# A graph layer in fp32: every gather of node rows is given a bound on its indices

## What is computed

```python
ea  = edge_attr @ w_e + b_e                        # (E, 64) @ (64, 256)
msg = relu(x[src] + ea)                            # one row of x per edge
agg = segment_sum(msg, dst, num_segments=N)        # sum of a node's edges
t = x + agg
h_local = bn(relu(t @ w1 + b1) @ w2 + b2 + x)
# attention inside groups of 32 nodes, 4 heads of 64 channels
q, k, v = split(x.reshape(256, 32, 256) @ in_w.T + in_b)
h_attn = bn(softmax(q k^T / 8) v @ out_w.T + out_b + x)
out = h_local + h_attn
out = bn(out + relu(out @ m_w1 + m_b1) @ m_w2 + m_b2)
return layernorm(x + out)
```

## Time and profile before

| what | value |
|---|---|
| median of 3 runs | 1321.83 us (1321.43 to 1322.18) |
| profiled execution, first to last instruction | 1321.8 us |
| PE busy with matmuls | 1242.6 us, 94% |
| POOL busy | 970.7 us, 73% |
| DVE busy | 819.9 us, 62% |
| ACT busy | 552.5 us, 42% |
| mean granted clock of TensorE | 0.977 of full speed |

### The profile page before, as it was taken

One profiled execution on the slowest core, in us unless ns is written; L12 is line 12 of the kernel. 1 busy time (PEld: TensorE's weight loads), 2 busy tenths in 40 slices (PEclk: granted clock), 3 DMA queues, 4 the chain that ended last, 5 costly groups with the idle time before them and its releaser, 6 DMA issues.

```text
span 1321.8 us, 21000 instructions
## 1 busy us (share of the span) xinstructions
PE 1242.6 (94%) x7307; PEld 729.6 (55%) x7307; DVE 819.9 (62%) x1831; ACT 552.5 (42%) x1077; POOL 970.7 (73%) x1032
## 2 busy tenths in 40 slices
PE   5797999999999999999999999999999999999997
PEld 3454555555555555555555545555455556767676
DVE  4757456657475575746667475575746657548554
ACT  1343434444344434444443444443444434444443
POOL 7777777777777777777777777777777777777760
PEclk7897999999999999999999999999999999999999
DMA  9454645555555555555555555555555555545540
GB/s 325 137 177 144 180 136 160 170 173 177 158 155 168 170 169 162 177 160 162 170 162 177 152 156 167 170 170 155 162 176 164 168 158 155 184 146 151 178 140 18
DMA packets 113259, 216.02 MB, mean 163 GB/s; under 512 B 21505, under 2 KB 62721, under 8 KB 113153
## 3 DMA queue, kind: packets, MB, share of 16 engines
q0 software_dynamic: 49152, 134.28, 35.1%
q1 hardware_dynamic: 62560, 77.09, 18.1%
q10 hardware_dynamic: 1440, 3.29, 0.7%
HBM read 197.80 MB, written 16.78 MB: 162 GB/s over the span
## 4 chain that ended last, share of the span: by engine, by line
PE 55%; POOL 19%; DVE 11%; issue 9%; DMA 4%; DVEq 1%; ACT 1%
PE bank L746 28%; POOL xg L368 19%; PE bank L774 12%; PE bank L789 11%; DMA xg<-in_x_dram,srcs 4%; DVE bank L592 3%; PE bank L798 2%; DVE mx L635 2%; DVE dif L640 1%; PE bank L871 1%; PE bank L845 1%; DVEq L608 1%; DVE o L667 1%; DVE aggT L624 1%; DVE probT L656 1%
## 5 line engine op out<-in xcount | busy, mean ns | idle before, releaser
L368 POOL DMA_INDIRECT xg<-in_x_dram,srcs x1024 | 969.8, 947 | 313.5 <-issue 297.0
L393 ACT ACTIVATE msg<-bank 128x512 f32<-128x512 f32 x512 | 277.7, 594 | 392.7 <-PE bank L774 392.2
L592 DVE TENSOR_TENSOR bank<-xg,bank 128x512 f32<-128x512 f32 x512 | 337.3, 690 | 157.8 <-DMA xg<-in_x_dram,srcs 132.4
L774 PE MATMUL bank<-we,ea 64*128 64x256 f32 x2048 | 297.8, 410 | 55.5 <-DVE bank L592 55.5
L774 PEld LDWEIGHTS bank<-we,ea 64*128 64x128 f32 x2048 | 182.0, 190 | 205.4 <-issue 146.8
L789 PE MATMUL bank<-msg,onehot 128*64 128x256 f32 x2048 | 254.7, 392 | 4.0 <-DVE aggT L624 4.0
L789 PEld LDWEIGHTS bank<-msg,onehot 128*64 128x64 f32 x2048 | 139.8, 139 | 103.7 <-issue 47.8
L624 DVE TENSOR_TENSOR aggT<-bank,aggT 128x128 f32 x256 | 74.7, 292 | 187.4 <-PE bank L798 142.7
L746 PE MATMUL bank<-xT,iwT 128*128 128x512 f32 x256 | 125.8, 614 | 6.6 <-DMA xT<-in_xT_dram 6.6
L746 PE MATMUL bank<-o,m 128*128 128x512 f32 (+2 forms) x352 | 122.8, 483 | 0.0
L746 PE MATMUL bank<-h,m 128*128 128x512 f32 (+2 forms) x352 | 116.8, 479 | 1.0 <-ACT h L453 1.0
(11 more groups left out here) (88 smaller groups left out, 927.0 us busy)
## 6 DMA issues: line engine op xcount, KB each, us to landing
ea<-in_ea_dram SPq DMA_DIRECT2D x128, 256.0 KB
xg<-in_x_dram,srcs POOLq DMA_INDIRECT x1024
xT<-in_xT_dram SPq DMA_DIRECT2D x32, 256.0 KB, 3.9
aggT<-in_xT_dram SPq DMA_DIRECT2D x32, 256.0 KB, 5.0
oT_dram<-oT SPq DMA_DIRECT2D x32, 256.0 KB
xn<-in_x_dram SPq DMA_DIRECT2D x32, 256.0 KB, 5.1
out_dram<-xn SPq DMA_DIRECT2D x30, 256.0 KB, 2.8
m<-in_m_dram ACTq DMA_DIRECT2D x2, 512.0 KB, 17.9
```

Of the source, the lines that this page charges most:

```text
L368: pool.indirect_dma_start(xg[:, q % NX, n * C:(n + 1) * C], None, t["x"], bass.IndirectOffsetOnAxis(k.srcs[:, at:at + 1], 0)).then_inc(s_x ...
L393: nc.scalar.activation(msg[:, q % NM, :], EA[q % 4][:, :], ACT.Relu).then_inc(s_msg, 1)
L592: nc.vector.tensor_tensor(EA[q % 4][:, :].rearrange("p (a c) -> p a c", a=2), xg[:, q % NX, :].rearrange("p (a c) -> p a c", a=2), KB[:, 0 ...
L774: ins = nc.tensor.matmul(EA[(2 * d + pair) % 4][:, two * C:(two + 1) * C], ea[rows, n % NEA, at:at + P], k.we[rows, :], start=False, stop= ...
```

## The change

Each gather in the loop of POOL is given `bounds_check=N - 1`, that is 8191, and `oob_is_err=False`: an index above 8191 is left out of the transfer, with no error raised. Before, no bound was given, and `oob_is_err` had its default, true. No index is above 8191, so nothing is left out. Buffers, order, waits and all other engines stay.

```diff
                     pool.indirect_dma_start(
                         xg[:, q % NX, n * C:(n + 1) * C], None,
                         t["x"],
-                        bass.IndirectOffsetOnAxis(k.srcs[:, at:at + 1], 0)
+                        bass.IndirectOffsetOnAxis(k.srcs[:, at:at + 1], 0),
+                        bounds_check=N - 1, oob_is_err=False
                     ).then_inc(s_xg[q % NX], 16)
```

## The result

The changed kernel takes 1373.84 us (median of 4 runs, 1372.88 to 1374.57) against 1322.01 us (1321.43 to 1322.33): a ratio of 1.0392, 95% interval 1.0379 to 1.0405. It is 51.8 us slower. The forecast was 1348.0 us, with a range from 1308 to 1447 us; the profiled span grew from 1321.8 to 1372.8 us, by 51.0 us.

What follows compares the result with a forecast made beforehand. POOL's gathers, a full conveyor at 1.252 us each, were taken as the bound where DVE waits for them. 872 x 0.03 = 26.2 us on 1321.8 us gave 1348.0 us, range 1308 to 1447 us.

Steps and rivals of the forecast that it cites:

- The bound of the kernel: Gathers on POOL: a full conveyor, 1024 x 1.252 = 1282 us of 1321.8 us, despite its 73% busy share.
- d: What one gather on POOL becomes longer, from its start to the next one's start; taken as 0.03 us.
- the slack: At the end, the last seed's lag behind its gather beyond a waiting seed's: 6.4 - 1.9 = 4.5 us.
- What d does to the end: End moves by the larger of 872 x d and 1024 x d - 4.5 us; both 26.2 us.
- the first rule: Gathers before the last DVE seed that waits, near 1097.84 us: end moves by at least 872 x d.
- The price of d: Per gather, 0.03 us: one instruction through POOL's sequencer, and a quarter of a 0.127 us whole pass over the indices.
- The wait that moves: Ahead of each gather, the free-buffer wait moves to the register move in front; costed at nothing.
- Hidden: Rival: move read under the running gather, comparison made anyway; d below 3 ns, time 1321.8 us; chance 0.27.
- A pass of its own: Rival: inside each gather, POOL goes over the 128 indices again, up to 0.127 us; up to 1447.3 us; chance 0.16.
- The error path goes away: Rival: gathers lose 0.03 us of error bookkeeping; gain 13.7 us over 455 gathers, to 1308.1 us; chance of faster 0.14.
- Cut-up transfers: Rival: gathers' queue goes from 48 to 144 packets per gather; beyond 1600 us; 0.07 together with a much slower gather.
- The signs to look for: Line of gathers: gap above 0.30 us means the move or its wait; median above 946 ns means the check.

## Why the prediction was right, and where it was off

**The bound of the kernel.** Right. POOL at 73% busy was a full conveyor, and d x 1024 less a part of the slack came out at the end.

**What d does to the end.** Right. With the measured d of 0.053 us, 1024 x 0.053 - 4.5 = 49.8 us; the span grew by 51.0 us. The slack gave back 3.5 us, not 4.5, since the last seed stayed 2.9 us behind its gather and not 1.9. The run with the bound on the early gathers bears out the first rule, 46 us expected and 45 measured. The late ones show that the slack swallows a part, 3.5 us expected and 4.9 measured in the repeat; as in the changed kernel, it seems to give back less than 4.5 us.

**The price of d.** This term was mis-sized: 0.03 us taken, 0.053 us measured, 26 us forecast and 51 us found. The reason that carried it was mostly wrong in kind. It was the price of one more instruction through the sequencer. The moves do cost 29 ns each, close to the spacing of the memsets, but they lie under the gathers; with one move in place of 1024 the time is the same. The price is inside the gather and nearly fixed. The second reason, a fraction of the 0.127 us that stood for a pass, pointed at the right place, but the fraction of a quarter was picked and not read from a row; it came out as 0.4. (The 0.127 us were not the smallest instruction of that shape either: the memsets of 128x1 take 0.10 to 0.12 us.) That the forecast got half of the change, and not none of it, is luck: a move and a bound have prices of like size.

**The wait that moves.** Costed at nothing, and nearly so. One reading behind it doesn't hold: the gaps that DVE ends are not gathered in the last 200 us of the gathers, where there are 10 of the 48 (3.3 of 14.8 us), and none of them is longer than 0.4 us. The wait stands on moves that run many gathers ahead. It shows once: the first gather starts at 3.9 us where it started at 3.4 us, 0.5 us. With one move and the wait on the gather it starts at 3.3 us, with the error kept, where the wait is on a move again, at 4.0 us.

**The rivals.** *Hidden*: half right. The mechanism that I gave for it holds for the move, and the Trainium skill's rule ("Perfetto Trace Analysis", DMA Instruction — SWDGE (GPSIMD)), that the sequencer is free once the DMA is pushed on, agrees with the trace: the last move runs 15.7 us ahead of its gather. But the comparison was not free, 52 ns where 3 ns would have decided. *A pass of its own*: the place was right, and the price lies within its 0.127 us. The argument of 1 ns more per row is out, but a pass over all indices at once would be a fixed price too, and no run tells it from other work inside the gather. *The error path goes away*: wrong, the flag alone changes nothing. Its judgement that shorter gathers gain little was sound: with gathers 39 ns shorter the kernel gained 12 us, where its sum would give 455 x 0.039 = 17.7 us. *Cut-up transfers*: wrong, 49152 packets as before (the 144 packets per gather were worked out from no row).

**The signs to look for.** The gap was to grow if the move was the price, the median if the check was. The median grew and the gap stayed. That pair of numbers puts the price inside the gather. That it is the bound and not the flag took the runs.

## What to carry to other kernels

Look at the distance from start to start on the engine that issues gathers: here a constant distance, with a gap of 0.30 us that no wait explains, meant that the engine was saturated, though its busy share read 73%. Then every nanosecond inside a gather counted about once for each gather, while a register move between two gathers counted nothing, since the sequencer ran ahead. A bound that no index can exceed was not free: where such an engine sets the time and the indices are known to be in range, try it without. Where a bound is needed, the silent form was the cheaper one here, but it leaves out a wrong index without a word.

## What the runs showed of the hardware that was not expected

- A gather's time on POOL depends little on its rows: 862 ns for 32, 900 to 907 for 64, 912 for 96, 946 for 128.
- A bound costs 37 to 52 ns, 42 at 32 rows and 52 at 128; the form that raises an error costs some 10 to 15 ns more than the silent one, though no index was ever beyond the bound.
- Rows that the bound leaves out save bytes (67.51 for 134.28 MB) but neither packets (49152) nor POOL's time (998 ns).
- POOL's sequencer passed a move with its gather in 0.55 us, and reached the last move 15.7 us before its gather ran.
